# Moving the attention state by pairs of batch rows on GpSimd, in a four-layer sequence kernel

## The reference

```
Q = einsum('bld,hde->bhle', X, W_Q);  K, V alike;  Q = xpos(Q);  K = xpos(K, downscale=True)
scores = einsum('bhle,bhme->bhlm', Q, K) * D        # D[n, m] = gamma_h ** (n - m) for n >= m, else 0
Y = einsum('bhlm,bhmv->bhlv', scores, V)
Yn = (Y - mean) * rsqrt(var + 1e-5);  Yn = Yn * gn_weight + gn_bias
G = X @ W_G;  out = (G * sigmoid(G) * Yn) @ W_O
x = layernorm(X + out)
```

## Time and profile before

| | before |
|---|---|
| median of 3 runs | 1226.98 us (1226.48 to 1228.27) |
| profiled execution, its own time | 1227.77 us |
| its span | 1226.0 us |
| PE, DVE, ACT, POOL busy | 90%, 79%, 50%, 40% of the span |
| attention layer, about | 0 to 284 us, a chunk in 29.6 us in the middle |
| state add L682 / multiplication L684, median of 32 | 734 / 730 ns |

### The profile page before, as it was taken

How to read it: one execution, slowest core, us unless ns; L and a number is a source line. 1 busy time by engine, 2 the same in 40 slices (tenths; PEclk the granted TensorE clock), 3 DMA queues, 4 the chain that set the end, 5 groups by cost and what they waited for, 6 DMA issues and landing times.

```text
span 1226.0 us, 16524 instructions
## 1 busy us (share of the span) xinstructions
PE 1100.8 (90%) x5776; PEld 847.8 (69%) x5776; DVE 965.9 (79%) x1416; ACT 611.3 (50%) x1047; POOL 489.9 (40%) x389
## 2 busy tenths in 40 slices
PE   6999999765999999999999999999999999995334
PEld 3566666544778777778778877877878887772223
DVE  3688888842004699899899899989989998998883
ACT  2344555522434535754665573565556457444453
POOL 1366666751434224424433432443443343331220
PEclk9999999967999999999999999999999999998657
DMA  6344445913342242234042333313404232310000
GB/s 219 107 146 164 164 163 194 323 64 105 101 133 76 87 137 87 60 113 138 22 134 79 110 88 100 120 53 110 142 36 120 86 103 70 103 52 0 0 18 17
DMA packets 45626, 126.99 MB, mean 104 GB/s; under 512 B 4352, under 2 KB 21504, under 8 KB 43136
## 3 DMA queue, kind: packets, MB, share of 16 engines
q1 hardware_dynamic: 44416, 114.72, 29.5%
q10 hardware_dynamic: 1152, 11.53, 2.6%
HBM read 117.85 MB, written 19.92 MB: 112 GB/s over the span
## 4 chain that ended last, share of the span: by engine, by line
PE 48%; DVE 23%; issue 3%; ACT 2%; POOL 1%; ACTq 0%; DVEq 0%; POOLq 0%
PE lower L1103 33%; PE bank L1103 14%; DVE tmp L1851 3%; DVE tmp L1841 2%; DVE Sq L1843 2%; DVE tmp L1857 2%; DVE delta L1853 2%; PE bank L1092 1%; DVE S L1859 1%; DVE stats L130 1%; DVE delta L1855 1%; DVE lower L2019 0%; DVE bank L2021 0%; DVE lower L2025 0%; DVE kvq L1822 0%
## 5 line engine op out<-in xcount | busy, mean ns | idle before, releaser
L1690 POOL TENSOR_TENSOR a_lo<-whole,a_hi 128x512 fp32r<-128x512 f32 x128 | 181.3, 1433 | 289.9 <-ACT a_hi L1372 197.1
L1103 PE MATMUL lower<-b_hi,ring 128*128 128x512 f32 x512 | 193.5, 396 | 1.4 <-ACT a_hi L1372 1.4
L1103 PE MATMUL lower<-a_hi,ring 128*128 128x512 f32 x512 | 192.3, 393 | 1.7 <-issue 1.7
L1103 PE MATMUL lower<-b_lo,ring 128*128 128x512 f32 x512 | 190.5, 390 | 1.7 <-POOL b_lo L1690 1.7
L1103 PE MATMUL lower<-a_lo,ring 128*128 128x512 f32 x512 | 190.3, 389 | 0.2 <-POOL a_lo L1690 0.2
L1690 POOL TENSOR_TENSOR b_lo<-whole,b_hi 128x512 fp32r<-128x512 f32 x64 | 94.0, 1476 | 146.1 <-ACT b_hi L1372 146.1
L1355 ACT ACTIVATE S<-S 128x1024 f32<-128x1024 f32 x56 | 58.6, 1058 | 183.0 <-DVE S L1859 183.0
L1371 ACT ACTIVATE whole<-lower,hs 128x512 f32<-128x512 f32 x128 | 87.7, 685 | 82.3 <-PE lower L1103 75.7
L421 PE MATMUL lower<-wa,xT 128*128 128x512 f32 x240 | 112.1, 611 | 10.0 <-DMA wa<-wa_dram 7.8
L1103 PEld LDWEIGHTS lower<-b_hi,ring 128*128 128x128 f32 x512 | 96.2, 188 | 21.9 <-issue 1.8
L1103 PEld LDWEIGHTS lower<-b_lo,ring 128*128 128x128 f32 x512 | 96.0, 188 | 22.0 <-POOL b_lo L1690 2.3
(11 more groups left out here) (252 smaller groups left out, 2375.2 us busy)
## 6 DMA issues: line engine op xcount, KB each, us to landing
ring<-ffn_copy_dram SPq DMA_DIRECT2D x128, 512.0 KB, 3.6
look<-ffn_dram ACTq DMA_DIRECT2D x8, 1408.0 KB, 5.9
ffn_copy_dram<-ffn_dram SPq DMA_DIRECT2D x8, 1408.0 KB, 8.6
xT<-xT_dram SPq DMA_DIRECT2D x8, 512.0 KB, 8.4
rope<-rope_dram SPq DMA_DIRECT2D x8, 512.0 KB, 8.9
xtok<-x_dram SPq DMA_DIRECT2D x8, 512.0 KB, 4.1
x1in<-x_dram SPq DMA_DIRECT2D x8, 512.0 KB, 4.9
x1res<-x_dram SPq DMA_DIRECT2D x8, 512.0 KB, 3.2
```

The lines of the kernel that those rows point to most:

```text
L1103: ins = nc.tensor.matmul(out, a, b, start=(first and n == 0), stop=(last and n == len(pairs) - 1))
L1690: nc.gpsimd.tensor_tensor(lo[:, m, :], t["whole"][:, m % 4, :], hi[:, m, :].bitcast(F32), ALU.subtract).then_inc(lo_done, 1)
```

## The change

`move_state` takes a half r in place of a row. One add and one multiplication of 128x512 stand where two of each with 128x256 stood; `decay` (128x256) is read twice through a broadcast over the two rows. The state is cleared by two memsets in place of four. The counts of `state_done` and `sum_done` are per pair. PE and ACT execute the same instructions as before, and wait for the same halves of the state.

```diff
@@ tensor, outputs(c, parity, r, follow)
-                    pe.wait_ge(state_done, c * BATCH + 2 * r + 2)
+                    pe.wait_ge(state_done, c * 2 + r + 1)
@@ scalar, first_copies(c, r)
-                        act.wait_ge(sum_done, (c - 1) * BATCH + 2 * r + 2)
+                        act.wait_ge(sum_done, (c - 1) * 2 + r + 1)
@@ gpsimd
-                for b in range(BATCH):
-                    nc.gpsimd.memset(state[:, b, :, :], 0.0).then_inc(state_done, 1)
+                for b in range(2):
+                    nc.gpsimd.memset(state[:, 2 * b:2 * b + 2], 0.0).then_inc(state_done, 1)
-                def move_state(c, b):
-                    pool.wait_ge(up_out, c * 2 + b // 2 + 1)
-                    st = state[:, b, :, :].rearrange("p g e -> p (g e)")
-                    nc.gpsimd.tensor_tensor(st, st, up[:, b], ALU.add).then_inc(sum_done, 1)
-                    pool.wait_ge(sum_done, c * BATCH + b + 1)
-                    nc.gpsimd.tensor_tensor(st, st, decay[:].rearrange("p g e -> p (g e)"),
-                                            ALU.mult).then_inc(state_done, 1)
+                def move_state(c, r):
+                    rows = slice(2 * r, 2 * r + 2)
+                    st = state[:, rows].rearrange("p b g e -> p b (g e)")
+                    kept = decay[:].rearrange("p g e -> p (g e)").unsqueeze(1).broadcast_to([P, 2, DIM])
+                    pool.wait_ge(up_out, c * 2 + r + 1)
+                    nc.gpsimd.tensor_tensor(st, st, up[:, rows], ALU.add).then_inc(sum_done, 1)
+                    pool.wait_ge(sum_done, c * 2 + r + 1)
+                    nc.gpsimd.tensor_tensor(st, st, kept, ALU.mult).then_inc(state_done, 1)
@@ gpsimd, body
                         gate_norm(c, parity, 0)
                         move_state(c, 0)
-                        move_state(c, 1)
                         gate_norm(c, parity, 1)
...
                     if attend:
-                        move_state(c, 2)
-                        move_state(c, 3)
+                        move_state(c, 1)
```

More of the change, by code:

```diff
@@ L659, in _ @@
                 nc.gpsimd.memset(inv_pow[:], -0.5).then_inc(pow_ready, 1)
-                for b in range(BATCH):
-                    nc.gpsimd.memset(state[:, b, :, :], 0.0).then_inc(state_done, 1)
+                for b in range(2):
+                    nc.gpsimd.memset(state[:, 2 * b:2 * b + 2], 0.0).then_inc(state_done, 1)
                 pool.wait_ge(pow_ready, 1)
-                pool.wait_ge(state_done, BATCH)
+                pool.wait_ge(state_done, 2)
                 pool.wait_ge(const_in, 16 * N_CONST)
```

## The result

| | before | after |
|---|---|---|
| median, 20 runs each | 1226.83 us | 1230.62 us (1228.04 to 1233.25) |
| ratio | | 1.0030 (95%: 1.0022 to 1.0037) |
| profiled execution, its span | 1227.77, 1226.0 us | 1232.38, 1230.6 us |
| first L421 that waits for DVE, chunk 1, to the same in chunk 6 | 147.85 us | 152.44 us |
| from there to the last store of the layer | 65.19 us | 65.44 us |

The changed kernel is slower by 3.8 us; 3.0 were forecast. The last two rows of time are from the profiled executions (71.27 to 219.12 and 284.31 us before; 70.53 to 222.97 and 288.41 after). They say where it went: into the middle of the attention layer (+4.6). The stretch ahead of the middle is 0.7 us shorter and the one behind the layer 0.5 longer; the first of these hangs on more than the change, since the middle begins anywhere from 69.5 to 71.5 us in the profiled runs of this document.

The account below looks back on a forecast made before the run. PE was taken to bound the kernel, with POOL's work looking free. 5 x 0.54 + 0.37 = 3.1 us, less about 0.1 in the first chunk, gave +3.0 and a forecast of 1230.0 us, range 1226.3 to 1232.0.

Parts of the forecast that it names:

- PE's slack at L753: Before each projection in chunks 1 to 6, PE waits about 0.1 us for DVE's L753, so it has no slack.
- Rival A: PE's slack at L753 takes z's delay; only POOL's saving in chunks 6 and 7 counts: 1226.0 us, chance 0.15.
- z and the turns: DVE's z (L793) takes turns with POOL's state add on SBUF; z lasts about 1.57 us in place of 1.03.
- +0.54 us per chunk: z ends 0.54 us later behind the longer add, and PE's next projection starts that much later: 5 x 0.54.
- a delay is kept, and not made good in the next chunk: Rgn hangs on DVE and PE work of the same body, so what PE loses to z stays lost.
- The second place, L755: POOL's gate_b comes first, L755 lasts about 1.6 us in place of 0.69; masked products stay covered by 0.3 us.
- Rival B: L755 is there before gate_b, DVE loses only 0.54 us, chunk 6 costs about 0.9 less: 1229.2 us, chance 0.20.
- Behind the second state move nobody waits: In the middle chunks POOL waits 0.80 us for DVE's variance anyway, so its 0.36 us saved per pair brings nothing.
- Chunk 6 and the end: PE loses 1.42 us in chunk 6; POOL's savings then count, shifting three roots by +1.03, +0.80 and +0.37 us.
- about 0.3 for the rest: +0.37 us at the last root, leading to the layer's end, with about 0.1 given back in the first chunk.

Follow-up runs that it names:

- x2: Changed kernel with only rows 0 and 1 moved by pair operations, rows 2 and 3 row by row: 1229.50 us, 1.0027 of the kernel before.
- x3: Rows 0 and 1 with two 256-column adds, then one 512-column multiplication; rows 2 and 3 row by row: 1227.50 us, 1.0006 of the kernel before.
- x7: Changed kernel with POOL's gate products of half 1 put ahead of the pair move of rows 0 and 1: 1226.12 us, 0.9997 of the kernel before.
- x10: Changed kernel with half 1's gate products first, no last-chunk state moves, and ScalarE's look sum behind the zT copies: 1221.29 us, 0.9965 of the kernel before.
- x11: Changed kernel with ScalarE's look sum and the load behind it moved after the zT copies: 1231.11 us, 1.0042 of the kernel before.
- x5: Kernel before, with DVE's look masking only 8 of 2816 columns: 1226.00 us, 0.9998 of the kernel before.
- x6: Changed kernel, with DVE's look masking only 8 of 2816 columns: 1227.84 us, 1.0016 of the kernel before.
- x8: Changed kernel without the two state moves of the last chunk: 1228.46 us, 1.0023 of the kernel before.
- x4: Rows 0 and 1 with one 512-column add, then two 256-column multiplications; rows 2 and 3 row by row: 1232.26 us, 1.0039 of the kernel before.

## Why the prediction was right, and where a term was off

**PE's slack at L753.** Right. All six waits rose, five of them from 0.34 to 0.9 us, and the neighbours kept theirs (34.1 us over 139). Rival A is out by that, and in x2 all six are 0.89 to 0.97.

**z and the turns.** Right, to 0.01 us: 1.57 forecast and measured. x3 shows that the instruction just ahead of z counts and not the total. The Trainium skill's page "SBUF — State Buffer", section "Who interferes with whom", has the one that issues first hold the shared port pair for its whole instruction; the traces agree, with z 0.69, 1.03 and 1.57 us behind nothing, a 256-column and a 512-column add.

**+0.54 us per chunk.** The size was off. The step that failed was that "a delay is kept, and not made good in the next chunk". From L421 to L421 chunks 2 to 5 of before take 29.62 us on average, and those of after 29.91 and 29.96 where the look keeps its turn: +0.3. Only chunk 1 to 2 shows the whole, 29.36 to 29.91. The rest went into a second path that I had not read. PE's L494 releases ScalarE, which goes through y, the look sum (2.56 us) and the look's load to v, gate and zT, and PE needs zT at L511. Before, that made v late; the ScalarE rows of the kernel before:

```profile
104.42 0.35 ACTq L609 DMA_DIRECT2D look<-ffn_dram  x1
104.89 0.37 ACT L561 COPY v<-lower 128x256 f32<-128x256 f32 x1 [0.63 <-PE lower L421]
```

PE's projection had ended at 104.33, 0.56 us ahead of v, and L511 waited (0.3 us at most, four times in the earlier trace rows's stretch). After, PE's projection ends at 104.14, and v follows at once:

```profile
103.60 0.35 ACTq L609 DMA_DIRECT2D look<-ffn_dram  x1
104.18 0.37 ACT L561 COPY v<-lower 128x256 f32<-128x256 f32 x1 [0.74 <-PE lower L421]
```

L494 comes before the wait for DVE, so this path is not delayed by it, and it had been the longer one by about 0.25 us. x7 shows it from one side (z freed, nothing gained), x10 and x11 from the other. So the five chunks gave 1.8 us (x2), not 2.7. Before, PE waited 0.20 to 0.29 us for zT in those four; 0.54 less that is the +0.3.

**The second place, L755.** Right: 1.62 us, gate_b first. Rival B is out. The masked products stayed covered in the middle, and rgn (105.31, idle 2.13 us for the variance) came later without PE noticing.

**Behind the second state move nobody waits.** So the prediction has it, and that put at nothing what stands at its front. Before, DVE's look started at 116.19 and POOL's add at 116.72. In chunk 2, counted from its own L421, the look came 0.15 us later in the changed kernel and the add, which waits for `up`, 0.39 us earlier. So of the 0.53 us between the two nothing is left in chunks 2 and 4, and the order is open there; in chunks 3 and 5 the look is ahead by 0.18 and 0.45 us. A lost turn costs 1.2 us of PE's time, in the one profiled run also 1.7 of clock. x5 and x6 show that with the look out of the way 1.8 us are left. How often it is lost in the timed runs is not known; the profiled ones had it 1 time (after), 2 (x8), 2 in part (x4), 0 (x2, x11). That it makes up the rest of the median's loss is the likeliest reading and not shown.

**Chunk 6 and the end.** Right up to the last root. L474's idle time before it went from 0.61 to 1.54 us. Counted from L421 of chunk 6, the three roots moved by +0.50, +0.24 and -0.31 us (241.89, 253.73 and 267.62, against the earlier trace rows); the forecast, less its 0.54 for chunk 6 itself, was +0.49, +0.26 and -0.17. But the last store came at +0.25, since from the last root to it took 20.79 us and not 20.23. PE's granted clock over that stretch was 0.58 on average after and 0.71 before. It goes up and down between 1.0 and 0.5 in this part of every profiled run, at other moments each time, so differences of some tenths in the column "end" are not to be read as the edit's; that the clock is all of these 0.56 us is not shown.

So two errors partly cancelled, and that the forecast of +3.0 came so near the measured 3.8 is in part luck. It was 2.7 for z, about 0.3 for the rest. The profiled 4.6 in the middle are 1.8 from z's wait and 2.8 from one lost turn; the median's 3.8 lie between.

## What to carry to other kernels

Where two engines take turns, the size of an instruction on the idle engine is a cost to the busy one: fusing two short operations saves issue time on the first and can lengthen the waits of the other, so look at what stands just ahead of the instruction on the path. Better, put there something that has to wait for that instruction anyway (x7). And before a delay is multiplied by the number of chunks, look for a second path into the same engine that is only a few tenths shorter; it caps the loss, and it also caps what removing the delay can give.

## What I had not expected of the hardware

One idle time of PE of 1.82 us in a busy stretch was followed by 0.50 of the clock (5.40 us for a projection of 3.70). In x8 the same idle time came twice (1.83 us both times) and the projections behind it ran at a granted clock of 1.00. What tells the two apart is open.

Who gets the turn can't be read from the recorded starts when these are 0.02 us apart. POOL's add lost to the look with a lead of 0.01 us (chunk 2 after), 0.01 and 0.02 (x11), and won with 0.02 twice (x8), 0.02 and 0.03 (x6) and 0.03 (chunk 4 after).
